# A six-sweep graph network: VectorE's operands moved to PSUM, the spread split in two, work shared with ScalarE

## The chip, the cores and the metric

One core of one Trainium2 chip runs the whole kernel. The metric is device time in microseconds, taken by the core; the median of several runs is given.

## The reference, cut to what matters

Four graph networks follow one another on 3125 nodes with 128 features and 100,000 edges sorted by destination. Before each stands a layer norm with a ReLU, behind each a residual add. Together they hold six attention layers over the edges:

```python
# L0, gat: 8 heads
e = leaky_relu(el[src] + er[dst], 0.01)
# L1, TransformerConv, twice: 4 heads; edge_attr = [cos((node_vec[src] - weight) * Wt + bt), edge_attr_64]
ed = edge_attr @ We
alpha = einsum(q[dst], k[src] + ed) / sqrt(32);  value = v[src] + ed
# L2: 4 heads
scores = einsum(q[col], k[row]) / sqrt(32);      value = v[row]
# L3, GATv2, twice: 8 heads
e = einsum(leaky_relu(xl[src] + xr[dst], 0.2), att);  value = xl[src]
# all of them
w = exp(e - segment_max(e, dst)[dst]);  w = w / segment_sum(w, dst)[dst]
out = segment_sum(w * value, dst)
```

Everything is float32.

## The kernel before, in words

A graph set-up is followed by seven node stages (matrix products over the nodes, norms, the joining of sums) with six edge sweeps between them. A sweep is `edge_sweep` (L539), called with a kind: `gat` (once), `tconv` (twice), `mha` (once), `gatv2` (twice). The change lies in this function alone.

The edges are cut into tiles of 128 edges, one edge per partition; `G` = 8 tiles are a group, and a sweep runs over `NG` = 98 groups. Per group i:

- GpSimd (`gather`, L733 to 741) issues eight indirect DMAs that fetch for 128 edges each the row of the source node (`rows`). There are four buffers; group i+2 is gathered in body i and waits for the messages of group i-2 and for an index tile that ScalarE copies (`indices`).
- SP loads eight windows of 128 destination rows (`qwin`), the marks of segment ends, and stores the sums.
- A one-hot matrix `hot` says which row of the window an edge belongs to. For gat and mha VectorE builds it by comparing `iota_free` with `rank_col` (`build_hot`, L973). For tconv and gatv2 ScalarE builds it as relu(1 - |iota - rank|): eight `measure` instructions (L780) and one Relu (L791). Except for gat it is bf16 first, and ScalarE casts it to float32 (`cast_hot`, L774).
- TensorE transposes it (`turn_hot`, L883), ScalarE copies that out of PSUM (`copy_hot`, L766), and TensorE multiplies it with the windows (`spread`, L886 to 904), which gives every edge its destination's row in PSUM. The two halves of a group have a PSUM bank each.
- VectorE makes the scores (`scores`, L1010 to 1043) with tiles `alpha`; for gat also the time angles (`angles`, L1045 to 1062), of which ScalarE takes the sine, TensorE the transposed form and SP the store to `attr_tab`, which tconv reads.
- TensorE transposes alpha (`turn_alpha`, L917). VectorE runs two scans along the edges and a subtraction (`maxima`, L988, L992, L997), ScalarE the exponential (L798), TensorE turns maxima and exponentials back (L909, L910), ScalarE copies them to the tile `pm` (`copy_probs`, L804), and VectorE multiplies them with the values (`messages`, L1070, L1071, L1075).
- TensorE sums the messages with `hot` (`sum_parts`, L928), ScalarE copies the sums (L810).

Each engine has one in-order queue, and its order inside body i is written out by hand in its own `body`. VectorE: maxima(i-1), scores(i), for gat angles(i), messages(i-1), build_hot(i+2). TensorE: turn_hot(i+1), two sum_parts of i-2, for gat turn_attr(i-3), turn_probs(i-1), the other sum_parts, turn_alpha(i), spread(i+1). ScalarE: exps(i-1), half of measure(i+2), copy_hot(i+1), two copy_parts(i-2), copy_probs(i-1), the other copy_parts, for gat copy_attr(i-3), else cast_hot(i+1), the rest of measure and build_hot(i+2), indices(i+3), and for gat in every other body two sines. All synchronisation is by counting semaphores.

Of the kernel before, what the change touches and what calls it, by code (L numbers as in the profile page):

```python
# [34 lines left out]
P = 128  # L35
# [503 lines left out]
def edge_sweep(nc, pl, sems, kind, H, tab, q_tab, part_tab, last_rows, scale, w):  # L539
# [22 lines left out]
    with ExitStack() as ctx:  # L562
# [8 lines left out]
        if kind != "gat":  # L571
            hot_b = [sb(f"hot_b{u}", [P, G, P], BF16) for u in range(2)]
# [4 lines left out]
        fwd = sb("fwd", [R, P])  # L577
# [3 lines left out]
        pm = sb("pm", [P, 2 * R])  # L581
        msg = sb("msg", [P, G, W])
# [11 lines left out]
        hot_ps = [pl.banks[0], pl.banks[2]] if kind == "gat" else [pl.banks[0][:, :].bitcast(BF16)]  # L594
        q_ps = [pl.banks[1], pl.banks[2]]
        e_ps = [pl.banks[3], pl.banks[4]]
        small = pl.banks[5]
        alpha_t = small[0:R, 0:P]
        prob_ps, max_ps = small[:, P:P + R], small[:, P + R:P + 2 * R]
# [21 lines left out]
        prob_copied = sem("prob_copied")  # L621
# [5 lines left out]
        STEPS = {"gat": 7, "gatv2": 4}.get(kind, 0)  # L627
        if kind in ("gat", "tconv"):
            attr_loaded = [sem(f"attr_loaded{u}") for u in range(S)]
        if kind == "gat":  # L630
            attr_stored = [sem(f"attr_stored{u}") for u in range(2)]
            angle_done = sem("angle_done")
            cos_done = sem("cos_done")
            attr_turned = sem("attr_turned")
            attr_copied = sem("attr_copied")
            tail_zeroed = sem("tail_zeroed")
        if kind == "tconv":
            e_used = sem("e_used")
        ring = [(i, i // S, i % S) for i in range(NG + 3)]
# [22 lines left out]
        with nc.Block() as block:  # L662
# [93 lines left out]
            def _(act):  # L756
                def indices(i, k, u, n):
# [4 lines left out]
                def copy_hot(i, k, u, n):  # L762
                    wait(act, hot_turned, i + 1)
                    per = G // len(hot_ps)
                    for h, bank in enumerate(hot_ps):
                        ins = act.activation(hot_t[:, h * per:(h + 1) * per, :],  # L766
                                             bank[:, 0:per * P].rearrange("p (t e) -> p t e", t=per), ACT.Copy)
                    ins.then_inc(hot_copied, 1)

                def cast_hot(i, k, u, n):  # L770
                    wait(act, hot_built, i + 1)
                    if n >= S:
# [12 lines left out]
                def build_hot(i, k, u, n):  # L785

                    wait(act, gap_done, i + 1)
                    if n >= 2:
                        wait(act, hot_turned, i - 1)
                        wait(act, hot_cast, i - 1)  # L790
                    act.activation(hot_b[u % 2][:, :, :], gap[:, :, :], ACT.Relu, scale=-1.0, bias=pl.one[:, 0:1]  # L791
                                   ).then_inc(hot_built, 1)

# [19 lines left out]

                def cosines(i, k, u, n):
                    wait(act, angle_done, i + 1)
                    if n >= S:
                        wait(act, attr_turned, 2 * (i - S + 1))
                    act.activation(attr[u][:, :, 0:64], ang2[u][:, :, :], ACT.Sin, bias=pl.half_pi[:, 0:1]
                                   ).then_inc(cos_done, 1)

                def copy_attr(i, k, u, n):
                    if n >= 2:
                        wait(act, attr_stored[u % 2], 16 * (2 * k + u // 2))
                    for h in range(2):
                        wait(act, attr_turned, 2 * i + h + 1)
                        act.activation(attr_t[u % 2][:, h * HALF * P:(h + 1) * HALF * P], e_ps[h][:, :], ACT.Copy
                                       ).then_inc(attr_copied, 1)

                def body(*g):
# [3 lines left out]
                    if act_builds and has(n, 2):  # L833
                        measure(*near(*g, 2), 0)
                    if has(n, 1):
                        copy_hot(*near(*g, 1))
                    if has(n, -2):
                        copy_parts(*near(*g, -2), 0)
                        copy_parts(*near(*g, -2), 1)
                    if has(n, -1):  # L840
                        copy_probs(*near(*g, -1))
# [3 lines left out]
                    if kind == "gat" and has(n, -3):  # L845
                        copy_attr(*near(*g, -3))
# [962 lines left out]
```

## Time and profile before

| | us |
|---|---|
| median of 3 runs | 9974.64 (9927.85 to 9978.87) |
| span of the profiled execution | 7290.4 |
| median less span | 2684.2 |
| VectorE busy in the span | 4893.6 (67 %) |
| GpSimd busy in the span | 5179.0 (71 %) |
| TensorE busy in the span | 4733.5 (65 %) |
| ScalarE busy in the span | 4079.6 (56 %) |
| mean granted TensorE clock | 0.792 |

The page of the profile gives the profiled execution's span, from its first to its last instruction, and no other time of that execution; so the table sets it beside the median of the runs. A busy share is over the whole span, in which the sweeps take the larger part and the node stages the rest. A GpSimd indirect DMA counts as busy while its descriptors are made, not while the data move.

### The profile page before, as it was taken

To read this page: it belongs to the slowest core of one execution; us is meant where nothing else is said; L and a number is where in the kernel's file an instruction comes from. 1 tells how busy PE (TensorE), PEld (TensorE's weight loads), DVE (VectorE), ACT (ScalarE), POOL (GpSimd) and SP (SyncE) were. 2 spreads that over 40 slices of the span, in tenths; PEclk is the share of its full clock that TensorE was granted. 3 is DMA by queue.
4 is the path that set the end of the run, shared out by engine and by line. 5 is a ranking of instruction groups with operands and counts; after the bars stand their busy time and mean duration, and the time that the engine had idled before them with its cause. 6 is when DMAs were issued, how large, how long until landed. Compare 5 with 4: busy or idle time off the path is not lost. (4 is left out here: it accounts for less than half of the span.)

```text
span 7290.4 us, 132506 instructions
## 1 busy us (share of the span) xinstructions
PE 4733.5 (65%) x30647; PEld 4262.1 (58%) x30647; DVE 4893.6 (67%) x9144; ACT 4079.6 (56%) x9739; POOL 5179.0 (71%) x5105
## 2 busy tenths in 40 slices
PE   2777776577777567777746666645666654666663
PEld 2677775466767457777635565535555553555553
DVE  5777886467777557777655555546777765777776
ACT  1555554466766457667623333326767654767672
POOL 4777774377777577777657777757777766777774
PEclk6777787788888778888868778867888876888886
DMA  2677775289998578898847777735555553555553
GB/s 71 183 192 194 194 196 157 69 251 258 259 261 256 154 219 258 255 261 255 228 116 208 206 203 206 206 102 148 159 159 159 159 139 97 159 159 159 159 159 88
DMA packets 1717674, 1334.47 MB, mean 183 GB/s; under 512 B 384948, under 2 KB 1559891, under 8 KB 1717524
## 3 DMA queue, kind: packets, MB, share of 16 engines
q1 hardware_dynamic: 1516788, 837.31, 40.0%
q0 software_dynamic: 200736, 495.45, 24.8%
q8 instruction: 59, 0.97, 0.1%
q14 instruction: 91, 0.75, 0.0%
HBM read 913.26 MB, written 418.79 MB: 183 GB/s over the span
## 5 line engine op out<-in xcount | busy, mean ns | idle before, releaser
L739 POOL DMA_INDIRECT s_rows<-kv_tab,s_idx x2352 | 2359.8, 1003 | 737.3 <-issue 703.8
L739 POOL DMA_INDIRECT s_rows<-xl_tab,s_idx x1568 | 1622.5, 1035 | 491.6 <-issue 476.8
L902 PE MATMUL bank<-s_qwin,s_hot_t 128*128 128x128 f32 (+1 forms) x9408 | 1657.2, 342 | 12.9 <-ACT s_hot_t L766 7.1
L928 PE MATMUL bank<-s_msg,s_hot 128*128 128x144 f32 (+1 forms) x9408 | 1553.5, 313 | 126.1 <-ACT s_part L810 90.9
L902 PEld LDWEIGHTS bank<-s_qwin,s_hot_t 128*128 128x128 f32 x9408 | 1557.9, 256 | 57.0 <-issue 31.0
L928 PEld LDWEIGHTS bank<-s_msg,s_hot 128*128 128x128 f32 x9408 | 1351.1, 211 | 189.0 <-ACT s_part L810 145.1
L917 PE MATMUL bank<-ident,s_alpha 128*32 128x128 f32 (+1 forms) x588 | 182.6, 310 | 1512.8 <-DVE s_alpha L1042 1506.1
L810 ACT ACTIVATE s_part<-bank 128x288 f32<-128x288 f32 (+1 forms) x2352 | 901.2, 403 | 352.5 <-PE bank L928 299.7
L917 PEld LDWEIGHTS bank<-ident,s_alpha 128*32 128x32 f32 (+1 forms) x588 | 62.6, 107 | 1598.6 <-issue 1598.4
L780 ACT ACTIVATE s_gap<-iota_free,rank_col 128x128 bf16<-128x128 f32 x3136 | 989.5, 387 | 0.1
L798 ACT ACTIVATE s_prob<-s_diff 32x128 f32<-32x128 f32 (+1 forms) x588 | 180.3, 307 | 1436.2 <-DVE s_diff L997 1407.5
L739 POOL DMA_INDIRECT s_rows<-gat_tab,s_idx x784 | 803.7, 1025 | 243.5 <-issue 238.6
L766 ACT ACTIVATE s_hot_t<-bank 128x1024 f32<-128x1024 bf16 (+1 forms) x686 | 605.4, 897 | 535.1 <-PE bank L883 514.8
L1030 DVE TENSOR_TENSOR s_rows<-s_rows,bank 128x1024 f32<-128x1024 f32 x392 | 476.6, 1216 | 593.6 <-DMA s_rows<-kv_tab,s_idx 437.9
L1071 DVE TENSOR_TENSOR s_msg<-s_rows,s_pm 128x1024 f32<-128x1024 f32 x588 | 716.4, 1218 | 0.0
L1040 DVE TENSOR_TENSOR s_prod<-bank,s_rows 128x512 f32<-128x512 f32 x588 | 405.4, 689 | 438.2 <-DMA s_rows<-kv_tab,s_idx 424.7
L1042 DVE TENSOR_REDUCE s_alpha<-s_prod 128x16 f32<-128x512 f32 (+1 forms) x980 | 672.1, 686 | 33.4
L1033 DVE TENSOR_TENSOR s_prod<-bank,s_rows 128x512 f32<-128x512 f32 x392 | 268.8, 686 | 577.6 <-DMA s_rows<-xl_tab,s_idx 577.6
L899 PE MATMUL bank<-We,s_attr_t 128*128 128x128 f32 x3136 | 548.7, 331 | 29.6 <-DMA s_attr_t<-attr_tab 12.2
L899 PEld LDWEIGHTS bank<-We,s_attr_t 128*128 128x128 f32 x3136 | 495.9, 241 | 69.2 <-issue 69.2
L774 ACT ACTIVATE s_hot<-s_hot_b 128x1024 f32<-128x1024 bf16 x490 | 513.6, 1048 | 0.0
L791 ACT ACTIVATE s_hot_b<-s_gap,one 128x1024 bf16<-128x1024 bf16 x392 | 450.1, 1148 | 24.4 <-ACT s_gap L780 14.2
(292 smaller groups left out, 6193.9 us busy)
## 6 DMA issues: line engine op xcount, KB each, us to landing
s_qwin<-q_tab SPq DMA_DIRECT2D x3920, 64.0 KB
part_tab<-s_part SPq DMA_DIRECT2D x294, 576.0 KB
part_tab<-s_part SPq DMA_DIRECT2D x294, 544.0 KB
s_attr_t<-attr_tab SPq DMA_DIRECT2D x196, 512.0 KB
attr_tab<-s_attr_t SPq DMA_DIRECT2D x98, 512.0 KB
s_rows<-kv_tab,s_idx POOLq DMA_INDIRECT x2352
s_rows<-xl_tab,s_idx POOLq DMA_INDIRECT x1568
s_attr<-in_edge_attr SPq DMA_DIRECT2D x97, 256.0 KB
```

What stands on the lines that cost most here:

```text
L739: pool.indirect_dma_start(out=rows[u][:, t, :], out_offset=None, in_=tab, in_offset=bass.IndirectOffsetOnAxis(ap=idx[u][:, t:t + 1], axis= ...
L766: ins = act.activation(hot_t[:, h * per:(h + 1) * per, :], bank[:, 0:per * P].rearrange("p (t e) -> p t e", t=per), ACT.Copy)
L774: act.activation(hot[u][:, :, :], hot_b[u % 2][:, :, :], ACT.Copy).then_inc(hot_cast, 1)
L780: ins = act.activation(gap[:, t, :], pl.iota_free[:, :], ACT.Abs, scale=-1.0, bias=pl.rank_col[:, bass.ds(i * G + t, 1)])
L791: act.activation(hot_b[u % 2][:, :, :], gap[:, :, :], ACT.Relu, scale=-1.0, bias=pl.one[:, 0:1]).then_inc(hot_built, 1)
L810: act.activation(part[u][:, PAIR * c:PAIR * (c + 1), :], part_ps[c % 2][:, 0:PAIR * W].rearrange("p (t w) -> p t w", t=PAIR), ACT.Copy).th ...
L899: pe.matmul(e_ps[h][:, (t - h * per) * D:(t - h * per + 1) * D], attr_t[u][:, t * P:(t + 1) * P], w["We"][:, :], start=True, stop=True)
L902: ins = pe.matmul(q_ps[h][:, (t - h * per) * QW:(t - h * per + 1) * QW], hot_t[:, t, :], qwin[u][:, t, :], start=True, stop=True)
L928: ins = pe.matmul(part_ps[c % 2][:, t * W:(t + 1) * W], hot[u][:, PAIR * c + t, :], msg[:, PAIR * c + t, :], start=True, stop=True)
L1030: v.tensor_tensor(kv, kv, bc(e.unsqueeze(2), [P, HALF, 2, D]), ALU.add).then_inc(e_used, 1)
L1042: v.tensor_reduce(alpha[:, t0:t1, :], prod[h][:, :, :].rearrange("p t (h c) -> p t h c", c=C), AX.X, ALU.add).then_inc(alpha_done, 1)
L1071: v.tensor_tensor(msg[:, :, 0:D].rearrange("p t (h c) -> p t h c", c=C), vals.rearrange("p t (h c) -> p t h c", c=C), bc(p.unsqueeze(3), [ ...
```

## The change

For every sweep:

- `messages` reads the turned exponentials and maxima straight from PSUM; the tile `pm`, `copy_probs` and its semaphore are gone, `turn_alpha(i)` waits for `msg_done` of i-1 instead, and `msg` has two buffers.
- The forward scan's result `fwd` lies in PSUM (bank 5).
- Constants that VectorE compares or multiplies with (`iota`, for gat also `Wt` and `bt`, for gatv2 `att`) are copied to PSUM bank 4 once ahead of the sweep.
- `spread` takes the half h as an argument; where there are two halves, the first stands ahead of `turn_alpha` on TensorE, the second behind it.

For gat: the one-hots are bf16 and cast by ScalarE, as in the other sweeps; the angle lies in PSUM; the fold (minimum of a and -a) becomes an Abs on ScalarE (`folds`) with a negative scale in the sine; VectorE's order becomes maxima, angles, messages, scores; turn_attr and copy_attr are split in halves with one bank.

For gatv2: VectorE adds in place in PSUM, ScalarE makes 0.2 times the sum (`slopes`, behind `copy_hot`), VectorE takes the maximum of the two, multiplies with att and reduces (`weigh`). The first four one-hots of a group are built by VectorE (`build_half`), the other four by ScalarE as before.

```diff
-                for h, bank in enumerate(hot_ps):
-                    ins = act.activation(hot_t[:, h * per:(h + 1) * per, :],
+                act.activation(hot_t[:, :, :], hot_ps[:, 0:G * P].rearrange("p (t e) -> p t e", t=G), ACT.Copy
+                               ).then_inc(hot_copied, 1)
...
+                def slopes(i, k, u, n):
+                    for h in range(2):
+                        wait(act, added, 2 * i + h + 1)
+                        act.activation(prod[h][:, :, :].rearrange("p t d -> p (t d)"), q_ps[h][:, :], ACT.Copy, scale=0.2
+                                       ).then_inc(slope_done, 1)
...
-                def copy_probs(i, k, u, n):
-                    wait(act, prob_turned, i + 1)
-                    if n >= 1:
-                        wait(act, msg_done, 3 * i)
-                    act.activation(pm[:, :], small[:, P:P + 2 * R], ACT.Copy).then_inc(prob_copied, 1)
...
+                def folds(i, k, u, n):
+                    wait(act, angle_done, i + 1)
+                    act.activation(ang2[u][:, :, :], ang2[u][:, :, :], ACT.Abs).then_inc(folded, 1)
...
                 def turn_alpha(i, k, u, n):
                     wait(pe, alpha_done, QB * (i + 1))
                     if n >= 1:
-                        wait(pe, prob_copied, i)
+                        wait(pe, msg_done, 3 * i)
...
+                    if QB == 2 and has(n, 1):
+                        spread(*near(*g, 1), 0)
                     if has(n):
                         turn_alpha(*g)
                     if has(n, 1):
-                        spread(*near(*g, 1))
+                        spread(*near(*g, 1), QB - 1)
...
-                    out = hot[u] if kind == "gat" else hot_b[u % 2]
-                    v.tensor_tensor(out[:, :, :], bc(pl.iota_free[:, :].unsqueeze(1), [P, G, P]),
+                    v.tensor_tensor(hot_b[u % 2][:, :, :], bc(iota_ps.unsqueeze(1), [P, G, P]),
...
+                def build_half(i, k, u, n):
+                    if n >= 2:
+                        wait(v, hot_turned, i - 1)
+                        wait(v, hot_cast, i - 1)
+                    v.tensor_tensor(hot_b[u % 2][:, 0:HALF, :], bc(iota_ps.unsqueeze(1), [P, HALF, P]),
+                                    bc(pl.rank_col[:, bass.ds(i * G, HALF)].unsqueeze(2), [P, HALF, P]),
+                                    ALU.is_equal).then_inc(half_built, 1)
...
+                def weigh(i, k, u, n, h):
+                    then = stepper(i, h)
+                    wait(v, slope_done, 2 * i + h + 1)
+                    t0, t1 = h * HALF, (h + 1) * HALF
+                    flat = prod[h][:, :, :].rearrange("p t d -> p (t d)")
+                    v.tensor_tensor(flat, q_ps[h][:, :], flat, ALU.max).then_inc(q_used, 1)
+                    wait(v, q_used, 2 * i + h + 1)
+                    then(v.tensor_tensor(prod[h][:, :, :], prod[h][:, :, :], bc(att_ps.unsqueeze(1), [P, HALF, D]), ALU.mult))
+                    v.tensor_reduce(alpha[:, t0:t1, :], prod[h][:, :, :].rearrange("p t (h c) -> p t h c", c=C),
+                                    AX.X, ALU.add).then_inc(alpha_done, 1)
...
                 def messages(i, k, u, n):
-                    wait(v, prob_copied, i + 1)
-                    if n >= 1:
-                        wait(v, part_done, NPAIR * i)
+                    out = msg[u % 2]
+                    wait(v, prob_turned, i + 1)
+                    if n >= 2:
+                        wait(v, part_done, NPAIR * (i - 1))
...
-                    p = pm[:, 0:R].rearrange("p (t h) -> p t h", h=H)
+                    p = prob_ps.rearrange("p (t h) -> p t h", h=H)
```

## Rows read from the trace of the kernel before

**Rows 1.** Sweeps as stretches: us; PE, PEld, DVE, ACT, POOL busy; clock, DMA share, GB/s.
```profile
158.90:1201.60 1042.70, 787.51 (x4913) 746.57 (x4913) 819.38 (x1643) 592.19 (x1244) 803.74 (x784) 0.76 0.71 190
1435.60:2458.00 1022.40, 763.50 (x5704) 704.08 (x5705) 720.88 (x1160) 707.21 (x1744) 783.81 (x784) 0.86 0.89 256
2597.00:3620.60 1023.60, 775.45 (x5725) 715.58 (x5726) 721.37 (x1161) 706.58 (x1744) 784.70 (x784) 0.86 0.89 256
3761.80:4791.90 1030.10, 667.45 (x4179) 607.85 (x4179) 593.00 (x1065) 379.94 (x869) 791.13 (x784) 0.80 0.72 204
4927.90:5979.20 1051.30, 666.54 (x4172) 605.50 (x4173) 757.01 (x1355) 730.16 (x1748) 812.17 (x784) 0.81 0.56 157
6120.80:7170.10 1049.30, 663.92 (x4160) 603.88 (x4161) 757.10 (x1355) 729.85 (x1745) 810.29 (x784) 0.81 0.56 158
```

**Rows 2.** GpSimd's gathers among the groups of instructions: busy, mean ns, idle before and releasers.
```profile
L739 POOL DMA_INDIRECT s_rows<-kv_tab,s_idx x2352 | 2359.8, 1003 | 737.3 <-issue 703.8 <-ACT s_idx L760 33.4
...
L739 POOL DMA_INDIRECT s_rows<-xl_tab,s_idx x1568 | 1622.5, 1035 | 491.6 <-issue 476.8 <-ACT s_idx L760 14.9
...
L739 POOL DMA_INDIRECT s_rows<-gat_tab,s_idx x784 | 803.7, 1025 | 243.5 <-issue 238.6 <-ACT s_idx L760 4.8
```

**Rows 3.** The tile of the gathered rows: duration ns min/median/max, one line.
```profile
L739 POOL DMA_INDIRECT s_rows<-kv_tab,s_idx x2352: 942/946/2015, 1435.6 to 4790.6; - x196
```

**Rows 4.** Timeline of GpSimd in a tconv sweep: start us, duration us.
```profile
1518.27 1.74 POOL L739 DMA_INDIRECT s_rows<-kv_tab,s_idx  x1 [0.30 <-issue]
...
1527.82 0.95 POOL L739 DMA_INDIRECT s_rows<-kv_tab,s_idx  x1 [0.30 <-issue]
```

**Rows 5.** Timeline of VectorE in the same stretch.
```profile
1517.97 1.22 DVE L1071 TENSOR_TENSOR s_msg<-s_rows,s_pm 128x1024 f32<-128x1024 f32 x1
...
1527.94 1.21 DVE L1071 TENSOR_TENSOR s_msg<-s_rows,s_pm 128x1024 f32<-128x1024 f32 x1
```

**Rows 6.** VectorE's groups of instructions, as in rows 2.
```profile
L1040 DVE TENSOR_TENSOR s_prod<-bank,s_rows 128x512 f32<-128x512 f32 x588 | 405.4, 689 | 438.2 <-DMA s_rows<-kv_tab,s_idx 424.7
...
L1036 DVE SCALAR_TENSOR_TENSOR s_prod<-s_prod 128x512 f32<-128x512 f32 x392 | 271.4, 692 | 13.4
...
L1033 DVE TENSOR_TENSOR s_prod<-bank,s_rows 128x512 f32<-128x512 f32 x392 | 268.8, 686 | 577.6 <-DMA s_rows<-xl_tab,s_idx 577.6
...
L1055 DVE TENSOR_SCALAR s_turns<-s_ang 128x512 f32<-128x512 f32 x98 | 41.9, 427 | 3.3
```

**Rows 7.** Timeline of VectorE in a gatv2 sweep, one group.
```profile
5513.16 0.69 DVE L1042 TENSOR_REDUCE s_alpha<-s_prod 128x32 f32<-128x512 f32 x1
5513.77 0.18 DVE L1070 COPY s_msg<-s_pm 128x64 f32<-128x64 f32 x1
...
5515.00 0.22 DVE L1075 TENSOR_TENSOR s_msg<-s_pm,last_col 128x64 f32<-128x64 f32 x1
5515.13 0.40 DVE L988 TENSOR_TENSOR_SCAN s_fwd<-s_neg,bank 64x128 f32<-64x128 f32 x1
...
5516.02 0.28 DVE L997 TENSOR_TENSOR s_diff<-bank,s_seg_max 64x128 f32<-64x128 f32 x1
```

**Rows 8.** Timeline of TensorE in the same stretch.
```profile
5506.77 0.61 PE L883 MATMUL bank<-ident_b,s_hot_b 128*128 128x128 bf16 x8
...
5513.99 0.40 PE L917 MATMUL bank<-ident,s_alpha 128*64 128x128 f32 x1 [3.96 <-DVE s_alpha L1042]
5514.24 3.78 PE L902 MATMUL bank<-s_qwin,s_hot_t 128*128 128x128 f32 x16
5517.82 1.06 PE L883 MATMUL bank<-ident_b,s_hot_b 128*128 128x128 bf16 x8
```

**Rows 9.** Timeline of ScalarE in the same stretch.
```profile
5518.91 1.02 ACT L766 ACTIVATE s_hot_t<-bank 128x1024 f32<-128x1024 bf16 x1 [1.10 <-PE bank L883]
```

**Rows 10.** ScalarE's groups of instructions, as in rows 2.
```profile
L791 ACT ACTIVATE s_hot_b<-s_gap,one 128x1024 bf16<-128x1024 bf16 x392 | 450.1, 1148 | 24.4 <-ACT s_gap L780 14.2 <-issue 0.2
...
L826 ACT ACTIVATE s_attr_t<-bank 128x512 f32<-128x512 f32 x196 | 106.0, 599 | 0.4 <-PE bank L943 0.4
```

More of the change, by code:

```diff
@@ L832, in body @@
                         exps(*near(*g, -1))
-                    if act_builds and has(n, 2):
+                    if kind == "tconv" and has(n, 2):
                         measure(*near(*g, 2), 0)
@@ L836, in body @@
                         copy_hot(*near(*g, 1))
+                    if kind == "gatv2" and has(n):
+                        slopes(*g)
                     if has(n, -2):
@@ L839, in body @@
                         copy_parts(*near(*g, -2), 1)
-                    if has(n, -1):
-                        copy_probs(*near(*g, -1))
+                    if kind == "gat" and has(n, -3):
+                        copy_attr(*near(*g, -3), 0)
                     if has(n, -2):
@@ L845, in body @@
                     if kind == "gat" and has(n, -3):
-                        copy_attr(*near(*g, -3))
-                    if kind != "gat" and has(n, 1):
+                        copy_attr(*near(*g, -3), 1)
+                    if has(n, 1):
                         cast_hot(*near(*g, 1))
@@ L856, in body @@
                             if has(n, d):
+                                folds(*near(*g, d))
+                        for d in (-2, -1):
+                            if has(n, d):
                                 cosines(*near(*g, d))
@@ L960, in body @@
                             sum_parts(*near(*g, -2), c)
+                    if kind == "gat" and has(n, -3):
+                        turn_attr(*near(*g, -3), 1)
+                    if QB == 2 and has(n, 1):
+                        spread(*near(*g, 1), 0)
                     if has(n):
@@ L1090, in body @@
                             v.memset(attr[(NG - 1) % S][:, :, 64:D], 0.0).then_inc(tail_zeroed, 1)
-                    if has(n, -1):
-                        messages(*near(*g, -1))
+                        if has(n, -1):
+                            messages(*near(*g, -1))
+                        if has(n):
+                            scores_gat(*g)
+                    else:
+                        if has(n):
+                            for h in range(2):
+                                scores(*g, h)
+                        if kind == "gatv2" and has(n, 2):
+                            build_half(*near(*g, 2))
+                        if kind == "gatv2" and has(n):
+                            for h in range(2):
+                                weigh(*g, h)
+                        if has(n, -1):
+                            messages(*near(*g, -1))
                     if not act_builds and has(n, 2):
                         build_hot(*near(*g, 2))
+                if not act_builds:
+                    ins = v.tensor_copy(iota_ps, pl.iota_free[:, :])
+                    if kind == "gat":
+                        v.tensor_copy(Wt_ps, w["Wt"][:, :])
+                        ins = v.tensor_copy(bt_ps, w["bt"][:, :])
+                    ins.then_inc(const_ready, 1)
+                    v.wait_ge(const_ready, 1)
+                if kind == "gatv2":
+                    v.tensor_copy(iota_ps, pl.iota_free[:, :])
+                    v.tensor_copy(att_ps, w["att"][:, :]).then_inc(const_ready, 1)
+                    v.wait_ge(const_ready, 1)
+                    build_half(0, 0, 0, 0)
+                    build_half(1, 0, 1, 1)
                 if not act_builds:
```

199 lines of the change are left out of this document (96 added, 103 removed).

## The prediction

> **What bounds the kernel now.** I read the six sweeps first as stretches: busy time of each engine from the first to the last gather of each [rows 1]. No engine is full there: GpSimd is busy 77 % (803.74 of 1042.70 us in the gat sweep), VectorE 79 %, TensorE 76 %. So I read, second, the groups of GpSimd's instructions with their idle time [rows 2]. Its 4704 row gathers wait for almost nothing: of 737.3 us idle before the kv gathers 703.8 is the fixed 0.30 us of issue, and only 33.4 us waits for an index tile (14.9 and 4.8 in the others). GpSimd is therefore never free: each gather is about 0.945 us (median) [rows 3] plus 0.30 us, so 8 gathers take 10.0 us and a sweep of 98 groups cannot run below 980 us. The measured periods, stretch over 98, are 10.64, 10.43, 10.44, 10.51, 10.73 and 10.71 us [rows 1]. VectorE, on the contrary, stands idle before the first read of the gathered rows: 577.6 us before L1033 over 196 groups, 2.9 us each [rows 6]. GpSimd sets the period.
>
> What lies between 10.0 us and the period is in the gathers themselves. Third, the two engines side by side [rows 4, 5]: the gather at 1518.27 takes 1.74 us; VectorE's L1071, with both inputs in SBUF (s_rows, s_pm), had begun at 1517.97 and ended at 1519.19, and the gather ended 0.82 us after that. The gather at 1527.82 began 0.12 us before the next L1071 and took its plain 0.95. So a gather pauses when, shortly after its start, a VectorE instruction with two SBUF inputs is running. The size of it, per sweep, is GpSimd busy less 784 x 0.945 = 740.9 us [rows 1, 3]: 62.9, 42.9, 43.8, 50.2, 71.3, 69.4, together 340 us. The Trainium skill says this too ("SBUF — State Buffer", Who interferes with whom): a VectorE instruction with two SBUF inputs blocks a GpSimd instruction that reads SBUF. The same section infers that descriptor generation needs only the write side and so would not be held by tensor_tensor; the 1.74 us row disagrees.
>
> **Profile against the clock.** The span is 7290.4 us, the timed median 9974.64. The profile gives no time of its own for the execution beyond the span, so 2684 us are placed by no row. I take them as lying around the span and unchanged, so that span differences carry over one to one; the other reading (timed executions run everything slower in proportion) is a rival.
>
> **The change part by part.**
>
> 1. *PSUM operands.* In every sweep the one-hot row numbers, Wt, bt, att, the forward scan, the turned probabilities and maxima, and the angle are read from PSUM. Of the sweep's VectorE instructions that had two SBUF inputs (L1071, L1075, L992, L981, L1036, L1037, L1052, L1054, L1057, L1058, L1061) none keeps them; only two small ones in gat (L1020, L1051) do. If the pause is what I say, 340 us of it can go. I leave 5 us in gat for those two.
>
> 2. *Cost of the PSUM reads.* L1040 (one input in PSUM) takes 689 ns, L1036 (both in SBUF) 692 ns for the same 128x512 [rows 6]: zero. L1055 loses the double rate it has from SBUF, 427 ns [rows 6], and goes to about 690: +0.26 us in gat; L1061 (0.69) leaves VectorE there. VectorE's writes into PSUM and PSUM reads that repeat one element (probabilities over their channels) are in no row: from 0 (nearest row, L1040) to a doubling of the instruction, which is what separates L1055 from 690 ns. I take 0. The Trainium skill ("VectorE: DVE Perf Modes", the TRN2 errata) gives PSUM sources 120 cycles of fixed cost against 58, an estimated 65 ns an instruction; by it gatv2's loop below would be some 0.6 us longer and the time about 9,800. The two rows just named do not show it.
>
> 3. *copy_probs gone, turn_alpha waits for messages.* ScalarE saves a small copy a group. But TensorE's L917 for group i now comes only when messages(i-1) is done, where it stood beside them, and VectorE's next scan waits for it. From the rows of one gatv2 group: L1042 ran from 5513.16 to 5513.85, L917 from 5513.99 for 0.40 [rows 7, 8]. So 0.14 + 0.40 and some 0.06 until the scan, 0.6 us of VectorE idleness a group. Behind L917 are queued half of the spread and turn_hot. Its cover is VectorE's present idleness, and in gat and mha build_hot (1024 elements, as long as an L1071) stands in between.
>
> 4. *Loops of the first four sweeps.* VectorE's busy time a group [rows 1] plus that 0.6: tconv 720.88/98 = 7.4, so 8.0 us; mha 593.00/98 = 6.1, so 6.7; gat 819.38/98 = 8.4, less 0.69, plus 0.26, so 8.0 with its wait covered and 8.6 without. All are under 10.0, so GpSimd keeps the period. Each half of the spread in tconv has its own slack: half stands ahead of L917 and is done when the scores begin. DMA's share in tconv is 0.89 at 10.43 us [rows 1] and becomes 0.93: no bound yet.
>
> 5. *gatv2.* VectorE adds build_half, 512 elements, 0.69 us, and needs a ScalarE scaling between its add and its max. ScalarE makes it after copy_hot, copy_hot after turn_hot, turn_hot after the second half of the spread, that after L917. With t = 0 at the end of messages (L1075, 5515.22): L917 ends at 0.54; the spread begins 0.25 after L917's start, at 0.39, and half of its 3.78 lasts to 2.3; turn_hot takes 0.61 or, at a lower clock, 1.06, to 2.9 or 3.3 [rows 8]; copy_hot 1.02, to 3.9 or 4.3 [rows 9]; scaling 0.6 (nearest row: a 128x512 copy from PSUM, 599 ns [rows 10]), to 4.5 or 4.9. VectorE has the scans from 0.6 to 1.8 (5515.13 to 5516.30 before [rows 7]), two adds and build_half, 0.7 each, to 3.9, so it stalls 0.6 to 1.0. Then six instructions at 0.72 apart (3 x 0.72 twice, the last reduce overlapped: 4.15), and messages 1.45 (5513.77 to 5515.22 [rows 7]): 10.1 to 10.5 us, and 9.6 if the stall is nil. I take 10.2, between GpSimd's 10.0 and the middle of the longer chain (10.5 would cost 59 us more); what is late next there is the scaling, no longer the gather. ScalarE's own work there falls: it loses half of the measures, half of the 1.15 us Relu [rows 10] and a copy, and gains two scalings of 0.6, so it is not itself the bound.
>
> 6. *gat on ScalarE.* Adds cast_hot (about 1.05, by copy_hot's 1.02 [rows 9]) and the Abs (0.6 to 0.7, by L826 [rows 10]), removes the small copy: 592.19/98 = 6.0 [rows 1] goes to at most 7.7 us. Hidden by the period of 10.0. The bf16 transposes shorten TensorE. Constants copied to PSUM ahead of each sweep and a longer drain: +1 us a sweep.
>
> **The sum.** gat 62.9 - 5 = 58; tconv 43 + 44; mha 50; gatv2 (10.73 - 10.2 + 10.71 - 10.2) x 98 = 102; less 6: 291 us. The span goes to about 7,000 and the time to 9974.64 - 291 = 9,684 us. All stalls gone and gatv2 at 10.0 would give 9,640.
>
> **The rivals.**
> A. *Proportional time.* Timed executions run everything slower, by 9974.64/7290.4 = 1.37. For: nothing in the trace accounts for 2684 us. Against: nothing in the trace shows such slowness either. Then 291 becomes 398: 9,577 us.
> B. *The gatv2 loop grows.* ScalarE or TensorE comes 0.5 us later than my chain (turn_hot waits for two engines' halves, TensorE's clock is 0.81 there [rows 1]) or each PSUM operand costs a little. The period stays at 10.7, the 102 us go: 9,786. Tightness of step 5 speaks for it, the 2.9 us of VectorE idleness against.
> C. *No gain.* The pause has another cause than the second SBUF input (the gather's own, or only the write side), or timed executions are not paced by GpSimd. Then 9,975 to 9,985. Against it: the end 0.82 us after L1071.
> D. *Slower.* Repeated-element PSUM reads run slower by p per 1024 elements. gatv2 has no slack and gets 2p a group (messages, and the two att products of 512 elements), 392p in all; gat gets 3p (messages, one-hots, Wt and bt) with 10.0 - 8.6 = 1.4 us of slack. At a doubling of the 1.22 us instruction [rows 5] less its fixed part, p = 1.07: gatv2 392 x 1.07 = 420, gat 98 x (3.2 - 1.4) = 177 on top; 9,684 + 597 = about 10,280. It turns the sign from p = 0.62 (686p = 291 + 137). For it: no row has such a read. Against: L1040 at full rate.
>
> **How the numbers follow.** Forecast 0.56, A 0.15, B 0.14, C 0.09, D 0.06. Likeliest: 9,684. Range: below to A and somewhat under, 9,530; above past B, 9,880. A measurement of this kernel tells about 0.5 % (50 us) from no change. Faster (forecast, A, B) 0.85; same (C and the small end of D) 0.09; slower 0.06.
>
> **What would show it.** Gathers at a median of 0.945 us with the total beyond 784 x 0.945 a sweep near zero: step 1. GpSimd stretches of 980 to 985 us in gat, tconv and mha, about 1,000 in gatv2. L1033's idleness for the gather in gatv2 nearly gone and idleness for ScalarE's scaling (about 0.5 us) in its place: step 5. About 0.6 us before the first scan in tconv: step 3. VectorE messages at 1.22 us against 2.3 tells D. Gathers that still take 1.7 us show step 1 wrong; a span that falls by 291 and a time that falls by 400 shows A.

## The result: two per cent slower here, four per cent faster on another chip

The changed kernel took 10,163.47 us (median of 4 runs, 10,151.35 to 10,174.74) against 9,961.99 for the kernel before: ratio 1.020, with a 95% interval of [1.0172, 1.0227], clear of 1. The forecast of 9,684 us and its range were wrong, and so was the sign. The span of the profiled execution is 10,172.9 us, and that execution's own time 10,174.74: nothing lies outside the span.

The sweeps of the changed kernel, as in [rows 1] (us; PE, PEld, DVE, ACT, POOL busy; clock, DMA share, GB/s):

```profile
161.10:1585.70 1424.60, 885.51 (x4832) 799.12 (x4833) 773.03 (x1526) 691.61 (x1221) 744.94 (x784) 0.63 0.50 137
1841.70:3392.40 1550.70, 890.88 (x5663) 796.74 (x5664) 718.03 (x1146) 688.76 (x1636) 741.00 (x784) 0.72 0.57 168
3543.40:5115.20 1571.80, 879.89 (x5626) 789.34 (x5626) 709.94 (x1134) 683.67 (x1624) 741.05 (x784) 0.72 0.56 166
5280.30:6650.40 1370.10, 632.49 (x4136) 574.94 (x4136) 598.53 (x1057) 354.47 (x762) 740.93 (x784) 0.72 0.53 153
6800.80:8349.80 1549.00, 712.17 (x4133) 637.96 (x4134) 803.69 (x1436) 636.48 (x1441) 739.66 (x784) 0.68 0.37 106
8506.80:10040.80 1534.00, 701.16 (x4118) 629.89 (x4118) 802.11 (x1436) 632.46 (x1434) 739.51 (x784) 0.68 0.37 107
```

GpSimd's busy time did fall, to within about 4 us of 784 x 0.945 us in every sweep, and its gathers from kv_tab and xl_tab last 945 and 943 ns against 1003 and 1035 in [rows 2]. Yet each sweep is 340 to 550 us longer than in [rows 1]. GpSimd now waits for ScalarE's index tile, which came to 53 us in all in [rows 2]:

```profile
POOL s_rows L745 <- ACT s_idx L768: 3139.1, 401, 14.3
```

(us in total, times, longest.) The other engines are late too. Inside the six sweeps VectorE, ScalarE and TensorE stand idle all three together for 5 us or more 126 times, 1139 us in all; in the execution behind [rows 1] that happens not once. A timeline of all engines in a tconv sweep (start, duration; in brackets the idle time before and its releaser):

```profile
2511.02 0.02 SPq L686 DMA_DIRECT2D s_attr_t<-attr_tab  x1
2511.80 0.27 PE L916 MATMUL bank<-s_qwin,s_hot_t 128*128 128x128 f32 x1 [0.45 <-issue]
2512.47 0.94 POOL L745 DMA_INDIRECT s_rows<-kv_tab,s_idx  x1 [0.30 <-issue]
2513.20 0.36 PE L916 MATMUL bank<-s_qwin,s_hot_t 128*128 128x128 f32 x1 [1.13 <-issue]
2513.90 0.40 ACT L817 ACTIVATE s_part<-bank 128x272 f32<-128x272 f32 x1 [6.95 <-issue]
2514.60 0.37 PE L916 MATMUL bank<-s_qwin,s_hot_t 128*128 128x128 f32 x1 [1.04 <-issue]
2515.30 1.43 PE L916 MATMUL bank<-s_qwin,s_hot_t 128*128 128x128 f32 x5 [0.33 <-issue]
2515.63 0.42 DVE L1008 TENSOR_TENSOR_SCAN bank<-s_neg,bank 32x128 f32<-32x128 f32 x1 [5.80 <-remote]
```

The eight matmuls of one half of the spread have no wait between them in the program. Yet three of them start singly, 1.40 us apart, and 0.70 us after the third the last five follow at once. Before its next instruction in these rows VectorE has been idle for 5.80 us, ScalarE for 6.95. In the whole trace 1836 of SyncE's register instructions (register moves and arithmetic) last between 0.65 and 0.75 us, where the execution behind [rows 1] has none over 0.1. So the page that I predicted from and the runs that were timed seem to show two conditions of the machine. The experiments tell them apart.

### The profile page after: what moved, and what is told of

Its sections match the earlier page's. It is cut to its first block and busy times, and to the rows that moved or that the text cites. A ratio compares the mean times of both kernels' runs of the same rounds, so it can differ in the third digit from the quotient of the medians.

```text
span 10172.9 us, 131177 instructions
## 1 busy us (share of the span) xinstructions
PE 5177.5 (51%) x30647; PEld 4557.3 (45%) x30647; DVE 4987.0 (49%) x9250; ACT 3970.5 (39%) x8857; POOL 4840.8 (48%) x5105
## 5 line engine op out<-in xcount | busy, mean ns | idle before, releaser
L941 PE MATMUL bank<-s_msg,s_hot 128*128 128x144 f32 (+1 forms) x9408 | 2080.3, 377 | 1834.1 <-ACT s_part L817 1316.1
L941 PEld LDWEIGHTS bank<-s_msg,s_hot 128*128 128x128 f32 x9408 | 1753.3, 261 | 2020.8 <-ACT s_part L817 1389.0
L1008 DVE TENSOR_TENSOR_SCAN bank<-s_neg,bank 32x128 f32<-32x128 f32 (+1 forms) x588 | 245.8, 418 | 2812.3 <-remote 2270.1
L772 ACT ACTIVATE s_hot_t<-bank 128x1024 f32<-128x1024 bf16 x588 | 594.8, 1012 | 1391.3 <-remote 1213.6
L897 PE MATMUL bank<-ident_b,s_hot_b 128*128 128x128 bf16 x4704 | 515.2, 258 | 856.4 <-issue 466.1
L897 PEld LDWEIGHTS bank<-ident_b,s_hot_b 128*128 128x128 bf16 x4704 | 394.4, 119 | 944.3 <-issue 637.3
L787 ACT ACTIVATE s_gap<-iota_free,rank_col 128x128 bf16<-128x128 f32 x2352 | 742.8, 388 | 0.1
L1100 DVE TENSOR_TENSOR s_msg<-s_rows,bank 128x1024 f32<-128x1024 f32 x588 | 711.3, 1210 | 0.0
L923 PE MATMUL bank<-ident,s_seg_max 32*128 32x32 f32 (+1 forms) x588 | 168.8, 287 | 785.5 <-ACT s_prob L811 594.0
L1056 DVE TENSOR_TENSOR s_prod<-bank,s_rows 128x512 f32<-128x512 f32 x588 | 404.1, 687 | 275.8 <-remote 219.3
```

What stands on the lines that cost most here:

```text
L772: act.activation(hot_t[:, :, :], hot_ps[:, 0:G * P].rearrange("p (t e) -> p t e", t=G), ACT.Copy).then_inc(hot_copied, 1)
L787: ins = act.activation(gap[:, t, :], pl.iota_free[:, :], ACT.Abs, scale=-1.0, bias=pl.rank_col[:, bass.ds(i * G + t, 1)])
L897: ins = pe.transpose(hot_ps[:, t * P:(t + 1) * P], hot_b[u % 2][:, t, :], pl.ident_b[:, :])
L941: ins = pe.matmul(part_ps[c % 2][:, t * W:(t + 1) * W], hot[u][:, PAIR * c + t, :], msg[u % 2][:, PAIR * c + t, :], start=True, stop=True)
L1056: v.tensor_tensor(prod[h][:, :, :], q, rows[u][:, t0:t1, 0:D], ALU.mult).then_inc(q_used, 1)
L1100: v.tensor_tensor(out[:, :, 0:D].rearrange("p t (h c) -> p t h c", c=C), vals.rearrange("p t (h c) -> p t h c", c=C), bc(p.unsqueeze(3), [ ...
```

## The experiments

Each group of runs went to one chip, with the kernel before beside it. Where that took about 7,295 us I speak of a free chip, where it took about 10,090 of a stalling one. A period is the time from the start of a sweep's first gather to the start of its last, per group of eight gathers. A pause is what the gathers of a sweep take beyond 784 x 0.945 us.

**1. Both kernels again, and the parts (free chip; before 7,294.58 us).**

> The kernel before, unchanged, profiled again. Its first profile had a span of 7290 us and gathers back to back, while its timed runs took 9962 us; the changed kernel's profile has the span of its timed runs (10173 us), index tiles that come late, and on SP register instructions of 0.7 us where the first profile has 0.03 to 0.04. Theory T (the timed executions are paced by something the first profile did not catch): span 9,900 to 10,000 us, periods of 14 to 16 us a group in all six sweeps, the same 0.7 us instructions, GpSimd waiting for ScalarE's index tile for 2,500 us or more. Rival R (only the changed kernel has these stalls): span near 7,290 us again, 10.4 to 10.7 us a group, and the 2,684 us lie outside the span.

7,290.9 us (the profiled execution 7,287.99, with a span of 7,286.2): the kernel before itself, 27 % under its first timed median. Time and span agree here too.

> The changed kernel with both halves of the spread behind turn_alpha again. If the half ahead of turn_alpha delays the scans and with them the loop over VectorE and TensorE (theory S), this is faster than the changed kernel's 10,163 us by 100 us or more. If the early half only fills TensorE's wait for the messages (rival), it is slower by 50 to 200 us: 10,210 to 10,360.

```diff
-                    if QB == 2 and has(n, 1):
-                        spread(*near(*g, 1), 0)
...
-                        spread(*near(*g, 1), QB - 1)
+                        for h in range(QB):
+                            spread(*near(*g, 1), h)
```

7,370.77 us, ratio 1.0099 [1.0077, 1.012]. Periods 10.0 to 10.17 in the first four sweeps, 11.66 in gatv2. VectorE in gatv2 (timeline as above):

```profile
5015.95 0.42 DVE L1007 TENSOR_TENSOR_SCAN bank<-s_neg,bank 64x128 f32<-64x128 f32 x1 [0.57 <-PE bank L931]
...
5017.88 0.70 DVE L1053 TENSOR_TENSOR bank<-bank,s_rows 128x512 f32<-128x512 f32 x1 [0.74 <-PE bank L916]
5019.59 0.70 DVE L1053 TENSOR_TENSOR bank<-bank,s_rows 128x512 f32<-128x512 f32 x1 [1.01 <-PE bank L916]
5020.19 0.68 DVE L1000 TENSOR_TENSOR s_hot_b<-bank,rank_col 128x512 bf16<-128x512 f32 x1
5021.98 0.69 DVE L1065 TENSOR_TENSOR s_prod<-bank,s_prod 128x512 f32<-128x512 f32 x1 [1.11 <-ACT s_prod L804]
```

This is the chain of step 5 with all of the spread in it: VectorE waits for TensorE before each add. Without the split the rest of the change loses 1 % on a free chip, though its gathers have no pauses left. The expectation spoke of a stalling chip; there this order was not run.

> The kernel before with the split spread alone: the first half ahead of turn_alpha, the second behind it. In that kernel turn_alpha waits for the scores only, and the half stands in its way. Theory S: slower than 9,962 us by 100 us or more. Rival: within 50 us of it, since the wait for the scores is long enough for the half to fit in.

The kernel before, with the two halves around turn_alpha: 7,274.59 us, ratio 0.9974 [0.9964, 0.9984], and the pauses of the gathers stay (337 us in the six sweeps, against 334 in the kernel before's run). Alone the split gives 20 us; it is what lets the PSUM operands pay.

> The changed kernel, with the turned maxima and exponentials of mha and gatv2 in PSUM bank 3 instead of 5, so that turn_alpha need not wait for the messages; turn_probs waits instead, where they are long done. gat and tconv keep the wait. Theory W (turn_alpha's wait for the messages lengthens the loop TensorE, VectorE, ScalarE): the three sweeps lose 1 to 1.5 us a group, 300 to 440 us, time 9,720 to 9,860. Rival (the loop is paced by stalls of the queues that are common to all engines, and 1.5 us more of waiting hides in them): within 60 us of 10,163.

```diff
+        own_bank = kind in ("mha", "gatv2")
+        back = pl.banks[3] if own_bank else small
+        prob_ps, max_ps = back[:, P:P + R], back[:, P + R:P + 2 * R]
...
-                    if n >= 1:
+                    if n >= 1 and not own_bank:
                         wait(pe, msg_done, 3 * i)
```

(turn_probs takes that wait in mha and gatv2.) 6,959.13 us, ratio 0.9546 [0.953, 0.9562], every period 9.99 to 10.03.

**2. The same on a stalling chip (before 10,090.34 us).**

> The changed kernel, unchanged, measured again beside the kernel before. In the last comparison the kernel before took 7,295 us instead of 9,962, with no 0.7 us instructions on SP; the result of the change (ratio 1.02) was measured while they were there. Theory C (the stalls are a condition of the chip, not of the change): if this run is free of them, the changed kernel takes 6,990 to 7,090 us (gat, tconv and mha at 10.0 to 10.2 us a group, gatv2 at 10.2 to 10.5) beside 7,295, ratio 0.96 to 0.97; if it has them, 10,100 to 10,200 beside 9,930 to 9,980. Rival (the changed kernel brings the stalls with it): 10,000 us or more beside 7,295.

10,245.45 us, ratio 1.0154 [1.0126, 1.0182]. The result repeats, and both kernels are slow here.

> The kernel before, unchanged, for its profile on the same chip as the changed kernel's. Free of stalls: 7,290 us and periods of 10.4 to 10.7 us. With them: 9,900 to 10,000 us, and then its sweeps show which of them are shorter than the changed kernel's 14.5, 15.8, 16.0, 14.0, 15.8, 15.7 us. By theory W (the wait of turn_alpha for the messages puts one more hop in the loop) all but gat are shorter by 0.3 to 1 us; by the rival (gatv2's new hop to ScalarE and back) only gatv2's two.

10,123.86 us (one execution), span 10,122.0. The kernel before has the stalls too: 1691 of SyncE's register instructions at 0.65 to 0.75 us, and 93 stretches, 685 us in all, in which the three engines stand together for 5 us or more. Its gat, first tconv, mha and two gatv2 sweeps, and GpSimd's wait:

```profile
161.30:1570.40 1409.10, 927.07 (x4837) 865.49 (x4837) 808.71 (x1614) 564.91 (x1221) 780.69 (x784) 0.69 0.52 139
1828.60:3405.50 1576.90, 896.02 (x5632) 791.92 (x5633) 717.90 (x1143) 703.29 (x1726) 758.27 (x784) 0.72 0.56 165
...
5301.90:6670.40 1368.50, 655.66 (x4093) 594.93 (x4093) 589.65 (x1046) 372.99 (x849) 766.99 (x784) 0.71 0.54 153
6828.00:8333.40 1505.40, 663.37 (x4118) 590.43 (x4118) 755.20 (x1335) 706.28 (x1729) 801.13 (x784) 0.72 0.39 109
8491.00:9992.10 1501.10, 658.63 (x4136) 585.08 (x4136) 757.40 (x1341) 709.39 (x1737) 802.62 (x784) 0.72 0.39 110
```

```profile
POOL s_rows L739 <- ACT s_idx L760: 2844.8, 406, 12.5
```

The gathers still pause (POOL busy 802 in gatv2), inside periods that GpSimd no longer sets. What the change takes out of them comes back as waiting for the index tile: 2844.8 here, 3180.3 in the changed kernel's trace on this chip (3139.1 in the first). The two kernels' periods on this chip, one execution each: gat 14.39 and 14.81, tconv 16.10, 16.13 and 16.08, 15.74, mha 13.97 and 14.15, gatv2 15.37, 15.33 and 15.69, 15.88. By these two executions the loss is in gatv2 (0.87 x 98 = 85 us), gat (41) and mha (18), while tconv gains 40. A sweep's period isn't steady there, though: the changed kernel's two traces on stalling chips differ by 0.13 to 0.31 us in each sweep. That the change loses rests on the interval of the timed runs; where it loses is less sure.

> The changed kernel with maxima and exponentials of mha and gatv2 in bank 3, again, beside the changed kernel on one chip. Free of stalls: 6,959 us as before, 30 to 130 us under the changed kernel. With stalls: by theory W mha and gatv2 gain 1 us a group or more over the changed kernel, 9,850 us or less; by the rival (the loop goes through ScalarE) within 60 us of it.

10,271.2 us, ratio 1.0174 [1.015, 1.0198], no less than the changed kernel's 10,245.45 beside it: turn_alpha's wait is not what costs there. This run shows a stall at its plainest, in gatv2:

```profile
7471.00 7.43 SPq L682 DMA_DIRECT2D s_qwin<-q_tab  x4
7472.85 0.94 POOL L747 DMA_INDIRECT s_rows<-xl_tab,s_idx  x1 [0.30 <-issue]
7473.16 0.42 DVE L1012 TENSOR_TENSOR_SCAN bank<-s_neg,bank 64x128 f32<-64x128 f32 x1 [10.83 <-remote]
...
7474.38 0.31 ACT L813 ACTIVATE s_prob<-s_diff 64x128 f32<-64x128 f32 x1 [12.16 <-issue]
```

SyncE takes 7.43 us to issue four of the windows. The same kernel on the free chip issues eight of them in 4.02 us:

```profile
5008.77 4.02 SPq L682 DMA_DIRECT2D s_qwin<-q_tab  x8
```

In this run's gatv2 sweeps every second group takes 21.5 us on average, the others 10.3 (from first scan to first scan). While VectorE, ScalarE and TensorE stand for 11 to 12 us, GpSimd gathers on at its full pace.

**3. The changed kernel on a free chip (before 7,297.44 us).**

> The changed kernel once more, to see it in the state of the chip in which the kernel before takes about 7,295 us. Theory (the plan of the prediction holds wherever the sequencers do not stall): where the kernel before takes 7,295 us, this takes 6,970 to 7,050 (ratio 0.955 to 0.967), with periods of 10.0 us in tconv and mha, 10.03 in gat and 10.0 to 10.5 in gatv2. Where the kernel before takes 9,960 to 10,120 us: ratio 1.015 to 1.023, gatv2 at 15.7 to 16.0 us. Rival (the changed kernel is slower in itself, whatever the chip's state): above 7,295 there too.

6,975.66 us, ratio 0.9559 [0.9543, 0.9575]. Its gat, first tconv, mha and first gatv2 sweep; its gathers; one gatv2 group of VectorE; and VectorE's idle time before L1066 over all gatv2 groups:

```profile
159.30:1150.70 991.40, 801.79 (x4857) 739.28 (x4858) 776.74 (x1537) 705.16 (x1230) 747.33 (x784) 0.72 0.74 198
1390.60:2372.50 981.90, 736.20 (x5714) 675.38 (x5715) 727.90 (x1158) 695.61 (x1648) 742.92 (x784) 0.93 0.91 267
...
3633.20:4615.60 982.40, 656.51 (x4174) 588.10 (x4175) 593.60 (x1065) 368.96 (x771) 743.33 (x784) 0.80 0.76 214
4750.40:5730.90 980.50, 632.49 (x4144) 578.19 (x4145) 808.41 (x1443) 645.91 (x1448) 741.36 (x784) 0.83 0.60 168
```

```profile
L745 POOL DMA_INDIRECT s_rows<-kv_tab,s_idx x2352 | 2230.1, 948 | 737.7 <-issue 679.6 <-ACT s_idx L768 29.7 <-DVE s_msg L1104 27.8
L745 POOL DMA_INDIRECT s_rows<-xl_tab,s_idx x1568 | 1483.2, 946 | 491.9 <-issue 459.3 <-ACT s_idx L768 17.9 <-DVE s_msg L1104 14.6
```

```profile
5014.16 0.68 DVE L1001 TENSOR_TENSOR s_hot_b<-bank,rank_col 128x512 bf16<-128x512 f32 x1
5015.88 0.69 DVE L1066 TENSOR_TENSOR s_prod<-bank,s_prod 128x512 f32<-128x512 f32 x1 [1.03 <-ACT s_prod L804]
...
5020.10 1.21 DVE L1100 TENSOR_TENSOR s_msg<-s_rows,bank 128x1024 f32<-128x1024 f32 x1
5021.23 0.22 DVE L1104 TENSOR_TENSOR s_msg<-bank,last_col 128x64 f32<-128x64 f32 x1
5022.02 0.42 DVE L1008 TENSOR_TENSOR_SCAN bank<-s_neg,bank 64x128 f32<-64x128 f32 x1 [0.57 <-PE bank L931]
```

```profile
L1066 DVE TENSOR_TENSOR s_prod<-bank,s_prod 128x512 f32<-128x512 f32 x392 | 268.7, 686 | 144.1 <-ACT s_prod L804 132.0 <-issue 11.6
```

The span falls from the 7,290.4 of the first profile to 6,974.4, by 316 us where the sum had 291.

> The changed kernel with the scaling by 0.2 back on VectorE in gatv2 (add into prod, maximum of prod and 0.2 prod in one instruction with both inputs in SBUF); build_half stays. Theory S (while the sequencers stall, the round trip VectorE to ScalarE to VectorE costs the gatv2 sweeps their 0.35 to 0.55 us a group): with the kernel before at 10,090 the gatv2 periods fall from 15.8 to about 15.4 and the time by 60 to 100 us, ratio about 1.007. Rival N (it is not this hop but the shared one-hots, or the gat sweep): no change beyond 20 us. Where nothing stalls: the two instructions pause the gathers again, 25 to 35 us a sweep, period about 10.3, 50 to 60 us more than the changed kernel.

```diff
-                        v.tensor_tensor(q, q, rows[u][:, t0:t1, :], ALU.add).then_inc(added, 1)
+                        v.tensor_tensor(prod[h][:, :, :], q, rows[u][:, t0:t1, :], ALU.add).then_inc(q_used, 1)
...
-                    v.tensor_tensor(flat, q_ps[h][:, :], flat, ALU.max).then_inc(q_used, 1)
+                    then(v.scalar_tensor_tensor(flat, flat, 0.2, flat, ALU.mult, ALU.max))
```

7,005.51 us, ratio 0.9597 [0.9581, 0.9613]: 30 us more than with the slopes, where 50 to 60 were expected. The pauses are 18.7 and 17.7 us in gatv2 (0.7 with the slopes), the period 10.19. That is less than the 25 to 35 us a sweep expected, of the right sign and in the right sweeps.

> As the run before it, and ScalarE builds all eight one-hots in gatv2 too: of the change to gatv2 only the operands in PSUM, turn_alpha's wait and the split spread are left. Theory H (sharing the one-hots, which makes TensorE and ScalarE wait for two engines, costs gatv2 while the sequencers stall): its periods fall by another 0.2 us or more. Theory S: no further change beyond 0.1 us. Where nothing stalls: 10.3 us a group as the run before it, or less by 0.1.

7,028.11 us, ratio 0.9634 [0.9618, 0.965]; pauses of 29.6 and 28.8 us, period 10.30. Sharing the one-hots is worth some 23 us on a free chip.

> The changed kernel with one operand put back in one sweep: in mha alone build_hot compares with iota in SBUF, not PSUM. Theory P (a VectorE instruction with two SBUF inputs holds a running gather): the time of the gathers beyond 784 x 0.945 us rises in mha from under 1 to 20 to 30 us (half of the kernel before's 50.8, for one of its two long instructions with two SBUF inputs), in the other five sweeps it stays as it was; where nothing stalls the mha period goes from 10.00 to 10.2 to 10.3. Rival (the pause came from something else that the change removed with it): under 3 us in mha too.

```diff
-                    v.tensor_tensor(hot_b[u % 2][:, :, :], bc(iota_ps.unsqueeze(1), [P, G, P]),
+                    iota = pl.iota_free[:, :] if kind == "mha" else iota_ps
+                    v.tensor_tensor(hot_b[u % 2][:, :, :], bc(iota.unsqueeze(1), [P, G, P]),
```

7,025.88 us, ratio 0.963. The mha sweep; the gathers of tconv and mha together against those of gatv2 (duration ns min/median/max); and build_hot itself, with `iota` in PSUM (gat) and in SBUF (mha):

```profile
3633.50:4660.00 1026.50, 664.66 (x4169) 595.15 (x4169) 594.69 (x1065) 371.10 (x770) 787.30 (x784) 0.80 0.72 205
```

```profile
L745 POOL DMA_INDIRECT s_rows<-kv_tab,s_idx x2352: 942/949/1976, 1391.1 to 4659.7; - x196
L745 POOL DMA_INDIRECT s_rows<-xl_tab,s_idx x1568: 941/947/988, 4796.5 to 6898.9; - x196
```

```profile
L994 DVE TENSOR_TENSOR s_hot_b<-bank,rank_col 128x1024 bf16<-128x1024 f32 x98 | 119.8, 1224 | 0.0
L994 DVE TENSOR_TENSOR s_hot_b<-iota_free,rank_col 128x1024 bf16<-128x1024 f32 x98 | 118.8, 1214 | 0.0
```

The instruction lasts as long either way. One operand moved back brings 47.1 us of pauses (2.6 before) into that sweep and none into another; its period goes from 10.03 to 10.48. The expectation was half of that size: this instruction alone nearly restores the 50 us that two long ones had caused, so pauses don't add up by instruction.

**4. What costs on a stalling chip.** The first three runs came to a free chip once more (before 7,292.37 us) and only repeat the group above, the last with a null result of its own.

> The changed kernel with the scaling by 0.2 back on VectorE in gatv2 once more, for the condition in which the kernel before takes 9,960 to 10,120 us. Theory S (there the round trip VectorE to ScalarE to VectorE costs gatv2 0.35 to 0.55 us a group): gatv2 periods of about 15.4 us, ratio about 1.007. Rival N: gatv2 at 15.7 to 16.0, ratio 1.015 to 1.02 as the changed kernel. If the kernel before takes about 7,295 us: ratio 0.96 again and nothing new.

7,001.29 us, ratio 0.9604.

> As the run before it, with ScalarE building all eight one-hots in gatv2. In the condition of 9,960 to 10,120 us. Theory H (sharing the one-hots costs gatv2 0.2 us or more a group there): gatv2 falls to 15.4 or below only here. Theory S: no further change beyond 0.1 us. If the kernel before takes about 7,295 us: ratio 0.963 again.

7,024.11 us, ratio 0.9636.

> The changed kernel with 16 more semaphore instructions a group (0.02 to 0.05 us each, nobody waits for them) on TensorE in mha and on ScalarE in gat. Theory I (in the slower condition an engine's queue is supplied with instructions too slowly, so that the time goes by their number): there the mha period rises from 14.0 to 14.1 us towards the 16 of tconv, whose TensorE has 75 instructions a group against 57, and the gat period from 14.6 to 15.2 or more. Rival (the stalls come at their own pace, whatever the queues hold): both stay within 0.2 us. Where the kernel before takes 7,295 us: 0.8 us of work in queues with slack, so both periods stay at 10.0 to 10.1 and the ratio at 0.956.

```diff
+        def extra(eng, kinds):
+            if kind in kinds:
+                for _ in range(4):
+                    eng.sem_inc(extra_passed, 1)
```

(called four times in a body, on ScalarE in gat and on TensorE in mha.) 6,978.53 us, ratio 0.9573 [0.9556, 0.959], mha at 10.00, gat at 10.15.

> The changed kernel without ScalarE's slopes and without the shared one-hots in gatv2, for a chip on which the kernel before takes 9,960 to 10,120 us. Theory S or H (one of the two costs gatv2 0.35 to 0.55 us a group there): gatv2 periods at 15.4 or below, ratio about 1.007. Rival N (it is neither; turn_alpha's wait or the gat sweep): gatv2 stays at 15.7 to 16.0, ratio 1.015 to 1.02. Where the kernel before takes 7,295 us: 0.963.

A stalling chip (before 10,081.24 us): 10,190.99, ratio 1.0105 [1.0074, 1.0135]. The gatv2 sweeps:

```profile
6833.20:8351.90 1518.70, 655.66 (x4093) 584.90 (x4093) 731.36 (x1328) 689.15 (x1630) 748.46 (x784) 0.70 0.37 108
8515.80:10035.00 1519.20, 672.98 (x4093) 602.83 (x4093) 733.54 (x1328) 692.51 (x1630) 749.87 (x784) 0.70 0.37 108
```

Period 15.51, between the kernel before (15.37, 15.33) and the changed one (15.66 to 15.88). So slopes and shared one-hots together would cost 0.15 to 0.37 us a group there, some half of gatv2's loss. But the same kernel's gatv2 periods differ by 0.13 and 0.22 us between two executions, and the interval of the ratio overlaps that of the changed kernel ([1.0126, 1.0182]) and that of the next run, so this is not settled.

> 16 more semaphore instructions a group on TensorE in mha and on ScalarE in gat, for such a chip. Theory I (time goes by the number of instructions in a queue there): mha from 14.0 to 14.1 towards 16, gat from 14.6 to 15.2 or more, the other sweeps as in the changed kernel. Rival (the stalls come at their own pace): both within 0.2 us. Where the kernel before takes 7,295 us: ratio 0.956 again.

10,268.6 us, ratio 1.0157 [1.0107, 1.0207]. The gat and mha sweeps, with 16 more instructions a group in ScalarE's and in TensorE's queue:

```profile
162.30:1642.30 1480.00, 925.41 (x4845) 829.60 (x4845) 773.98 (x1528) 694.89 (x1225) 745.05 (x784) 0.61 0.48 132
5360.00:6756.20 1396.20, 652.59 (x4093) 584.24 (x4093) 592.20 (x1047) 353.37 (x755) 740.83 (x784) 0.71 0.52 150
```

Beside the run before it on the same chip gat is at 15.11 against 14.88 and mha at 14.26 against 14.14, but tconv, which has nothing added, is at 16.05 against 15.81 as well. In mha a rise of 0.12 where theory I asked for up to 2 us lets it fall. Gat's 0.23 is no more than tconv's 0.24; against the changed kernel's 14.54 and 14.81 it is 0.3 to 0.6, more than the rival's 0.2, so for ScalarE's queue the run decides less.

## Why the prediction was wrong

*Profile against the clock* is the step that failed. I took the 2684 us between span and median "as lying around the span and unchanged", so that a shorter span would shorten the time one to one. In its place the runs show that span and time agree within 2 us, on free and on stalling chips, and that the missing time lies in the sweeps: on a stalling chip the six stretches of the kernel before add up to 8,941 us against 6,219 in [rows 1], with periods of 14.0 to 16.1 us, not 10.4 to 10.7. There GpSimd doesn't set the period, and the 291 us that the sum takes out of its gathers and of gatv2's loop gain nothing; the changed kernel loses 155 to 201 us. The profiled execution was of the free kind, and the first timed ones, which left no trace, by their times of the other. No row of the trace could show the stalls, but a gap of 27 % was a reason to doubt that trace and metric belong together.

*Step 1* held in both conditions. The pauses of all six sweeps were 340 us before and 15 after in the free kind, 220 and 2 in the stalling one. The run with `iota` back in SBUF shows the cause with one operand. The Trainium skill ("SBUF — State Buffer", Who interferes with whom) says that a VectorE instruction with two SBUF inputs contends with a GpSimd instruction that reads SBUF; the gather reads its index tile there, and the 47.1 us agree. The section's inference that tensor_tensor leaves descriptor generation alone does not fit them.

*Step 2* held: L1084 (L1055 before), which now reads PSUM, takes 691 ns where about 690 was said. L1100 takes 1210 ns against the 1218 of L1071, and L1066 686 with one PSUM input against the 692 of L1036 with none. The Trainium skill ("VectorE: DVE Perf Modes", the TRN2 errata) gives a PSUM source 120 cycles of fixed cost against 58; none of these tensor_tensor rows shows the difference. Rival D, a slow repeated read of PSUM, is out by L1100.

*Step 3*: 0.57 us before the first scan in the gatv2 group shown, where 0.6 was forecast; on average 0.56 in gatv2, 0.52 in tconv and next to none in mha, where build_hot stands in between as said. It is hidden on a free chip.

*Steps 4 and 6* held on a free chip: 10.03 in tconv and mha, 10.12 in gat.

*Step 5* was mis-sized: the stall for the slopes is there (1.03 us in the group shown, but 132.0/196 = 0.67 on average, at the low end of the 0.6 to 1.0 forecast), and the period is 10.01, not 10.2. The loop closes within GpSimd's 10.0. By the stretches the sweeps gain 51 us in gat (58 in the sum), 82 in tconv (87), 48 in mha (50) and 140 in gatv2 (102). So the sum of 291 for the measured 316 is near in part because errors of both signs meet in it.

*The rivals.* A asked the right question and gave the wrong form: the slower executions are not the same ones stretched. The changed kernel's gathers last 945 ns in them and 948 in the free ones, while its periods grow by half, and the kernel loses where A has it gain 398 us. C's second half, "timed executions are not paced by GpSimd", is what happened. C had a chance of 0.09 and an end of no change; a loss with that cause was in no rival.

*What stays open.* What makes the stalls, and why one chip has them and another not, is not shown. In the experiments no chip was seen in both conditions (2 and 14 were free, 14 in two groups of runs; 8 and 12 stalled), but each was seen for a short time only, and the chips of the first profile and of the first timed runs are not known. So the condition may also come and go with time. One rival stands untested: that the stalls belong to the recording of the execution. The traces of stalling executions hold 60,314 to 68,488 semaphore updates, the free ones 191,601 to 195,299, for the same programs (131,177 instructions in the changed kernel's traces of either kind). With so many missing, the releasers named in the stalling traces, the 2844.8 and 3180.3 us for the index tile among them, are less certain than those of the free ones. No run here sets an unrecorded execution beside a recorded one.

What costs the changed kernel its 1.5 to 2 % on a stalling chip is open as well. That some half of gatv2's loss goes with the slopes and the shared one-hots rests on one execution of each kernel and lies near the spread between executions. The split of the spread, the order on VectorE in gat and the Abs on ScalarE were not taken out there. No kernel run here beats the one before on a stalling chip. On a free one the changed kernel with its own bank is the fastest (0.9546), though its interval overlaps the changed kernel's.

## What to carry to other kernels

Before any sum, lay the profiled execution's span against the timed runs: where the two belonged together here they differed by 2 us. A gap of many per cent is a reason to suspect that the profile does not show what is being timed, and a gain in the engine that sets the pace there may be no gain in the metric. Where GpSimd's gathers set the pace, look for the VectorE instructions with two SBUF inputs. Moving one operand of a tensor_tensor to PSUM cost nothing in its duration here and took the pauses away; a tensor_scalar with its one input moved there went from 427 to 691 ns. A hop to another engine that hides behind a 10 us pace may have to be paid for where something else sets the pace; these runs suggest it and don't settle it.

## What was not expected of the hardware

- The same kernel takes 7,275 to 7,305 us on some chips and 9,928 to 10,135 on others; both are steady within a group of runs.
- On the second kind, 1691 to 2142 of SyncE's register instructions in an execution last 0.65 to 0.75 us (none on the first kind), and matmuls with no wait between them start 0.70 or 1.40 us apart. Inside the sweeps VectorE, ScalarE and TensorE stand together for 5 us or more 93 to 153 times, for up to 18 us (never on the first kind), while GpSimd's gathers in the changed kernel keep their 0.945 us.
- The granted clock goes with it: 0.93 in the changed kernel's first tconv sweep on a free chip, 0.72 on a stalling one.
- One VectorE instruction a group with both inputs in SBUF makes the gathers of a sweep 47.1 us longer; with one of the inputs in PSUM it is as long itself and they are not.
